# Two stages put in another order: the preparation of three weight sets before the image loop, and the third half band inside it

## The reference

```
x = x + wavelet_conv(group_norm(x), w0, w1, w2, bias)
x = x + similarity_conv(group_norm(x), spatial_weight)

wavelet_conv: three levels; each takes a 2x2 Haar transform of the low part,
  convolves the 128 stacked channels with its own 5x5 weights (128 x 128 x 25),
  and the inverse transforms add the levels up again
similarity_conv: a 5x5 neighbourhood; every neighbour is weighted by
  (cosine similarity over the channels + 1) / 2 * spatial_weight[tap]
```

## Time and profile before

| | us |
|---|---|
| median of 3 runs | 1970.23 |
| lowest and highest of them | 1963.1, 1977.1 |
| profiled execution | 1958.81 |
| its span, first to last instruction | 1957.2 |
| TensorE busy in it | 1624.4 (83%) |
| VectorE busy | 1364.0 (70%) |
| ScalarE busy | 748.6 (38%) |
| GpSimd busy | 428.0 (22%) |
| mean granted clock of TensorE | 0.915 of full speed |

### The profile page before, as it was taken

One profiled execution on the slowest core, in us unless ns is written; L12 is line 12 of the kernel. 1 busy time (PEld: TensorE's weight loads), 2 busy tenths in 40 slices (PEclk: granted clock), 3 DMA queues, 4 the chain that ended last, 5 costly groups with the idle time before them and its releaser, 6 DMA issues.

```text
span 1957.2 us, 52434 instructions
## 1 busy us (share of the span) xinstructions
PE 1624.4 (83%) x19071; PEld 884.2 (45%) x19071; DVE 1364.0 (70%) x1995; ACT 748.6 (38%) x1318; POOL 428.0 (22%) x760
## 2 busy tenths in 40 slices
PE   4868689799898889889888889888988888985686
PEld 3634244444444454444544444445444444442454
DVE  6433965986589766985599666985599557875553
ACT  2330135442445234432444244432544244423541
POOL 2333241302241222212040222212140223110000
PEclk8879889999999999999999999989999999897566
DMA  5332236755476626864576637673585547671664
GB/s 187 86 87 80 62 100 166 217 148 142 127 204 187 176 82 186 219 166 124 133 217 167 158 99 210 187 184 96 156 229 152 127 125 203 176 191 55 157 184 116
DMA packets 108649, 296.96 MB, mean 152 GB/s; under 512 B 24181, under 2 KB 57973, under 8 KB 107765
## 3 DMA queue, kind: packets, MB, share of 16 engines
q1 hardware_dynamic: 71408, 190.49, 36.9%
q0 software_dynamic: 36864, 101.47, 18.0%
HBM read 221.92 MB, written 69.94 MB: 149 GB/s over the span
## 4 chain that ended last, share of the span: by engine, by line
PE 49%; DVE 26%; issue 16%; ACT 5%; DVEq 2%; DMA 1%; POOL 1%; SPq 0%; ACTq 0%; POOLq 0%
PE conv L1283 13%; PE conv L1257 8%; PE gram L1348 8%; PE out_ps L1384 5%; DVE wgt L1019 4%; PE stat_ps L1306 4%; PE conv L1242 3%; PE vals_ps L1331 3%; PE out_ps L1373 2%; DVE st_s L970 2%; DVE st_a L967 2%; PE conv L1508 2%; DVE eo L835 2%; DVE xa L835 1%; DVE st_v L981 1%
## 5 line engine op out<-in xcount | busy, mean ns | idle before, releaser
L1283 PE MATMUL conv<-thl,wconv 128*128 128x496 f16 (+2 forms) x1920 | 514.8, 395 | 12.5 <-DVE xa L913 9.5
L1019 DVE SCALAR_TENSOR_TENSOR wgt<-gram,tapw 124x512 f32<-124x512 f32 x512 | 347.5, 682 | 224.2 <-PE gram L1348 189.2
L452 POOL DMA_DIRECT2D ring<-in_x x576 | 331.9, 582 | 340.1 <-ACT xa L524 251.0
L1348 PE MATMUL gram<-unit_mem 128*60 128x128 f16 x4096 | 251.5, 247 | 115.6 <-issue 54.8
L1348 PEld LDWEIGHTS gram<-unit_mem 128*60 128x60 f16 x4096 | 153.1, 113 | 321.2 <-issue 320.2
L1257 PE MATMUL conv<-thl,wconv 128*128 128x480 f16 (+7 forms) x1200 | 256.9, 368 | 0.0
L1283 PEld LDWEIGHTS conv<-thl,wconv 128*128 128x128 f16 x1920 | 159.3, 101 | 193.7 <-issue 39.4
L481 POOL DMA_DIRECT2D up<-d_z x128 | 69.3, 546 | 628.4 <-DVE xa L950 592.2
L524 ACT ACTIVATE thl<-tw 128x1024 f16<-128x1024 f32 x64 | 67.7, 1059 | 325.3 <-DVE tw L835 188.2
L1384 PE MATMUL out_ps<-wgt,vals 124*32 124x128 f32 x4096 | 182.1, 297 | 1.4 <-issue 0.8
L524 ACT ACTIVATE vals<-vals_ps 124x512 f32<-124x512 f32 x128 | 76.6, 598 | 258.5 <-PE vals_ps L1331 257.8
(11 more groups left out here) (140 smaller groups left out, 2073.1 us busy)
## 6 DMA issues: line engine op xcount, KB each, us to landing
unit_mem<-d_hl SPq DMA_DIRECT2D x128, 360.0 KB
unit_mem<-d_hl SPq DMA_DIRECT2D x256, 180.0 KB
ring<-in_x POOLq DMA_DIRECT2D x288, 128.0 KB, 2.7
ring<-in_x POOLq DMA_DIRECT2D x288, 127.0 KB, 2.8
d_hl<-st_hl SPq DMA_DIRECT2D x64, 360.0 KB
d_v<-st_v SPq DMA_DIRECT2D x64, 360.0 KB
unit_mem<-d_v SPq DMA_DIRECT2D x64, 360.0 KB
up<-d_z POOLq DMA_DIRECT2D x160, 128.0 KB, 2.6
```

The source lines that it names most:

```text
L452: pool.dma_start(dst, src).then_inc(raw_in[slot], 16)
L1019: V.scalar_tensor_tensor(out=dst, in0=g, scalar=SIM_SCALE ** 2, in1=tapw[:, :].unsqueeze(1).to_broadcast([KN, 2, 2 * QN]), op0=ALU.add, op ...
L1283: last = mm(dst[:, :, b0:b1], wconv0[:, w, 2 * (p % ROWS4) + s, dx + 2, :], thl[:, p % 2, d, s, :, b0 + dx:b1 + dx] if p % ROWS4 != 1 else ...
L1348: last = mm(bank[row:row + KQ, col:col + QN], key[:, q, e_at, TH * KW * g:TH * KW * g + KQ], tile[:, :, TH * g + 1:TH * g + 1 + TH, 1:1 + ...
```

## The change

- `wmix` is now three places: level 0's stays in `xa`, level 1's goes where `wraw[0]` lies, level 2's where `wraw[1]` lies. ScalarE writes into such a place once the raw weights there are mixed and their peak is found.
- TensorE's order becomes: one side of level 0, the first three tiles of its other side, one side of level 1, the other nine tiles of level 0, group-norm products of image 0, one side of level 2, levels 1 and 2 on the other side.
- VectorE's `peak(1)` moves behind level 0's first three tiles. The first four chunks' statistics move into level 0, the other four, the pad clearing and the group norm directly behind level 0, `peak(2)` behind these.
- ScalarE's `fill` of chunks 0 to 3 stands before level 2's half-mixed copies, `fill` of chunks 4 to 7 between the highs of levels 1 and 2. It waits for level 0's tiles alone.
- SP loads the tap table when level 1 is through (its place is level 1's half-mixed weights), instead of after level 0's first mix.
- In the loop ScalarE does `half_in` and `square_half` of half band 2 ahead of the copies of `up` and of half band 1's `count_own` and `unit_highs`, and three of the six norm pieces stand four to six matmuls later.

```diff
-NORMS_AT = [8, 20, 32, 50, 74, 92]
+NORMS_AT = [8, 20, 36, 54, 80, 92]
...
-        wmix = xa[:, :, :].rearrange("p a b -> p (a b)")[:, 0:TAPS * P]
-        wrow = [wmix[:, n * K * P:(n + 1) * K * P] for n in range(K)]
+        wmix = [xa[:, :, :].rearrange("p a b -> p (a b)")[:, 0:TAPS * P], wraw[0], wraw[1]]
+        wrow = [wmix[0][:, n * K * P:(n + 1) * K * P] for n in range(K)]
...
-            sp.wait_ge(wmixed, 7)
-            sp.wait_ge(wlevel, 1)
+            sp.wait_ge(wfull, TILES_BEFORE[2])
             sp.dma_start(tap_c, tapmask).then_inc(taps_in, 16)
...
                 if first(n):
-                    act.wait_ge(wfull, TILES_ALL)
+                    act.wait_ge(wfull, W0_TOTAL)
...
                     norms(b, 1, 0)
                     norms(b, 1, 1)
+                    half_in(b, 2)
+                    square_half(b, 2)
                 if conv:
 
                     act.wait_ge(up2_in, 64 * i + 64)
...
                     count_own(b, 1)
                     unit_highs(b, 1)
-                    half_in(b, 2)
-                    square_half(b, 2)
...
-            for n in range(3):
+            def keep_mixed(n):
                 for t in range(0, TAPS, 4):
                     m = min(4, TAPS - t)
                     k = 7 * n + t // 4
                     act.wait_ge(wmixed, k + 1)
                     if n > 0 and t == 0:
-                        act.wait_ge(wfull, TILES_BEFORE[n])
-                    copy(wmix[:, t * P:(t + m) * P], conv_ps[k % 2][:, 0:m * P]).then_inc(wmix_kept, 1)
+                        act.wait_ge(wlevel, 3 * n - 2)
+                    copy(wmix[n][:, t * P:(t + m) * P], conv_ps[k % 2][:, 0:m * P]).then_inc(wmix_kept, 1)
+
+            def highs(n, first_tile, end_tile):
...
+            keep_mixed(0)
+            highs(0, 0, 3)
+            keep_mixed(1)
+            highs(0, 3, W0_TOTAL)
+            root(gn1, gn1_var, gn1_root, 0)
+            for c in range(SLOTS):
+                fill(0, c)
+            keep_mixed(2)
+            highs(1, 0, 7)
+            for c in range(SLOTS, CHUNKS):
+                fill(0, c)
+            highs(2, 0, 7)
             act.wait_ge(const_in, 16 * 7)
-            root(gn1, gn1_var, gn1_root, 0)
-            for c in range(CHUNKS):
-                fill(0, c)
             opening(0)
...
+            level_scale(0)
...
+            dve.wait_ge(wmix_kept, 7)
+            combine(0, 0)
+            lows(0, tiles_of(0)[0:3])
+            peak(1)
+            combine(2, 1)
+            lows(0, tiles_of(0)[3:6])
+            dve.wait_ge(wfull, 6)
+            combine(3, 0)
+            for c in range(SLOTS):
+                raw_stats(0, c)
+            lows(0, tiles_of(0)[6:12])
+            level_scale(1)
+            dve.wait_ge(wfull, W0_TOTAL)
+            V.memset(xa[:, 0:2, :], 0.0)
+            V.memset(xa[:, H0 + 2:H0 + 4, :], 0.0)
+            V.memset(mean_conv, 0.0).then_inc(pads_clear, 1)
+            for c in range(SLOTS, CHUNKS):
+                raw_stats(0, c)
+            dve.wait_ge(const_in, 16 * 7)
+            gn_open(gn1, bn1, bn1_done, gn1_part, 0, CHUNKS)
+            gn_mean(gn1, gn1_chain, gn1_part, gn1_mm, 0)
+            gn_spread(gn1, gn1_mm, gn1_var, 0)
+            gn_close(gn1, gn1_chain, gn1_root, gn1_done, 0, X_SCALE)
+            peak(2)
+            level_scale(2)
+            lows(1, tiles_of(1))
+            lows(2, tiles_of(2))
...
+            mix_one_side(0)
+            level_products(0)
+            mix_both_sides(0, 0, 3)
+            mix_one_side(1)
+            mix_both_sides(0, 3, W0_TOTAL)
+            level_products(1)
             gn_products(gn1, gn1_part, gn1_mm, 0, 0)
             gn_products(gn1, gn1_part, gn1_mm, 0, 1)
+            mix_one_side(2)
+            level_products(2)
+            mix_both_sides(1, 0, 7)
+            mix_both_sides(2, 0, 7)
```

More of the change, by code:

```diff
@@ L738, in _ @@
                     if n > 0 and t == 0:
-                        act.wait_ge(wfull, TILES_BEFORE[n])
-                    copy(wmix[:, t * P:(t + m) * P], conv_ps[k % 2][:, 0:m * P]).then_inc(wmix_kept, 1)
+                        act.wait_ge(wlevel, 3 * n - 2)
+                    copy(wmix[n][:, t * P:(t + m) * P], conv_ps[k % 2][:, 0:m * P]).then_inc(wmix_kept, 1)
+            def highs(n, first_tile, end_tile):
                 act.wait_ge(wlevel, 3 * n + 3)
                 for k, (dst, scale) in enumerate(weight_tiles(n, 0), TILES_BEFORE[n]):
-                    act.wait_ge(wfull, k + 1)
-                    copy(dst, gram_ps[k % 2][:, 0:dst.shape[1]], scale=scale).then_inc(whigh, 1)
+                    if first_tile <= k - TILES_BEFORE[n] < end_tile:
+                        act.wait_ge(wfull, k + 1)
+                        copy(dst, gram_ps[k % 2][:, 0:dst.shape[1]], scale=scale).then_inc(whigh, 1)
+            keep_mixed(0)
[10 more added lines that the diff above has]
+            highs(2, 0, 7)
             act.wait_ge(const_in, 16 * 7)
-            root(gn1, gn1_var, gn1_root, 0)
-            for c in range(CHUNKS):
-                fill(0, c)
             opening(0)
@@ L1188, in _ @@
             peak(0)
-            for n in range(3):
-                level_scale(n)
-                if n == 0:
-                    dve.wait_ge(wlevel, 3)
-                    steps.link(dve, V.tensor_scalar(small[:, 7:8], wscale[0], 1 / 8, None, ALU.mult))
-                    steps.link(dve, V.tensor_scalar(small[:, 8:9], wscale[0], 1 / 32, None, ALU.mult))
-                    V.tensor_scalar(unscale_x, unscale[0], X_SCALE, None, ALU.mult)
-                    steps.link(dve, V.tensor_scalar(unscale_sq, unscale[0], unscale[0], None, ALU.mult))
-                if n < 2:
-                    peak(n + 1)
-                if n == 0:
-                    dve.wait_ge(wmix_kept, 7)
-                    combine(0, 0)
-                    lows(0, tiles_of(0)[0:3])
-                    combine(2, 1)
-                    lows(0, tiles_of(0)[3:6])
-                    dve.wait_ge(wfull, 6)
-                    combine(3, 0)
-                    lows(0, tiles_of(0)[6:12])
-                else:
-                    lows(n, tiles_of(n))
-                if n < 2:
-                    for c in range(SLOTS * n, SLOTS * n + SLOTS):
-                        raw_stats(0, c)
+            level_scale(0)
@@ new lines, in _ @@
+            dve.wait_ge(wlevel, 3)
+            steps.link(dve, V.tensor_scalar(small[:, 7:8], wscale[0], 1 / 8, None, ALU.mult))
+            steps.link(dve, V.tensor_scalar(small[:, 8:9], wscale[0], 1 / 32, None, ALU.mult))
+            V.tensor_scalar(unscale_x, unscale[0], X_SCALE, None, ALU.mult)
+            steps.link(dve, V.tensor_scalar(unscale_sq, unscale[0], unscale[0], None, ALU.mult))
+            dve.wait_ge(wmix_kept, 7)
+            combine(0, 0)
+            lows(0, tiles_of(0)[0:3])
@@ L1499, in _, with mix_one_side @@
             pe.wait_ge(zeroed, 4)
-            for n in range(3):
+            def mix_one_side(n):
                 w = wraw[n].rearrange("o (i t) -> o t i", t=TAPS)
@@ L1509, in _, with level_products @@
                     last.then_inc(wmixed, 1)
+            def level_products(n):
                 pe.wait_ge(wlevel, 3 * n + 1)
@@ L1516, in _, with mix_both_sides @@
                 last.then_inc(wlevel_mm, 1)
+            def mix_both_sides(n, first_tile, end_tile):
                 pe.wait_ge(wmix_kept, 7 * n + 7)
@@ L1521, in _ @@
                     sources = [(None, t) for t in range(0, TAPS, 4)]
-                for k, (kind, t) in enumerate(sources, TILES_BEFORE[n]):
+                for k, (kind, t) in enumerate(sources[first_tile:end_tile], TILES_BEFORE[n] + first_tile):
                     m = min(4, (TAPS if kind is None else 2 * K) - t)
@@ L1526, in _ @@
                     if kind is None:
-                        last = mm(gram_ps[k % 2][:, 0:m * P], mix, wmix[:, t * P:(t + m) * P], start=True, stop=True)
+                        last = mm(gram_ps[k % 2][:, 0:m * P], mix, wmix[n][:, t * P:(t + m) * P], start=True, stop=True)
                     elif kind == 1:
@@ L1531, in _ @@
                             at = s if s < K else (K - 1) * K + s - K
-                            last = mm(gram_ps[k % 2][:, (s - t) * P:(s - t + 1) * P], mix, wmix[:, at * P:(at + 1) * P],
+                            last = mm(gram_ps[k % 2][:, (s - t) * P:(s - t + 1) * P], mix, wmix[0][:, at * P:(at + 1) * P],
                                       start=True, stop=True)
```

8 lines of the change are left out of this document (removed).

## The result

| | before | after |
|---|---|---|
| median | 1966.66 (4 runs, 1952.63 to 1977.1) | 1903.92 (4 runs, 1897.99 to 1913.54) |
| ratio, 95% interval | | 0.971 (0.9642 to 0.9779) |
| profiled execution | 1958.81 | 1905.71 |
| its span | 1957.2 | 1904.2 |
| granted clock | 0.915 | 0.925 |

The change is faster by 2.9%. The direction was right and the size too small.

What follows compares the result with a forecast made beforehand. No engine alone sets the end (TensorE 49%, VectorE 26% of the chain of waits). Gains of 15 before the first image, 23.8 in seven iterations and 3.1 in iteration 8, 42 us, take 1970.2 to 1928, range 1914 to 1956.

Steps and rivals of the forecast that it cites:

- (a): Before the first image: `peak(1)` behind the first three low tiles brings TensorE's tile 2 to 28.9, gain 7.2 us.
- (b): Level 1's one-sided mix hides 11.3 us of VectorE, pays 2.2 us for low clock; TensorE back at level 0 at 44.1.
- (c): Rest of level 0 ends at 62, including 1 us for low clock; level scale and pads bring it to 63.8.
- (d): The second four chunks' reads start near 52.6, the last lands at 64.3; their four statistics end at about 66.3.
- (e): Group norm takes as long as before: first fill at 71.0; fill 3 awaits the ring's third read, ends at 77.1.
- (f): Level 2's one-sided mix, after a new wait behind ScalarE's copies and 1 us for the clock, ends at 87.0.
- (g): Other side of levels 1 and 2: level 1 until 96.8, fills 4 to 7 until 99.9, level 2 until 107.7.
- (h): Low-passes before the first image take 8.6, ending at 115.9; another 6.6 puts level 2's convolution at 122.5.
- Loop given back: Rival: the loop's eight steps are bound by VectorE and unit DMAs, 18 us of gain remain, 1952; chance 0.08.
- head nothing: Rival: the ring's third read and the ScalarE queue behind it swallow the gain before the first image, 1943; chance 0.08.
- Low clock throughout the head: Rival: one-sided mixes before the first image at half rate, head 15 us worse, loop 27 better, 1958; chance 0.06.
- ScalarE blocked at the new place of `half_in(2)`: Rival in the loop: ScalarE waits there on `unit_lows(0)`, some 12 us later than now, slower than before, 1990; chance 0.04.

Runs made afterwards that it cites:

- e5: The changed kernel with `peak(1)` back in front of level 0's first combination; 1919.07 us, ratio 0.98 to the kernel before.
- e2: The kernel before with only the loop's change, the old preparation kept; 1928.34 us, ratio 0.9863 to the kernel before.
- e8: The changed kernel, but SyncE loads unit 1 only when level 1's result is in memory (iterations 1 to 7); 1933.84 us, ratio 0.9897 to before.
- after_again: The repeat: the changed kernel measured once more, nothing altered; 1903.82 us, ratio 0.9743 to the kernel before.
- e10: The changed kernel with level 2's half-mixed copies ahead of fills 0 to 3 and the tap table's load behind chunk 7; 1900.16 us, ratio 0.9714 to before.
- e3: The changed kernel with the norm pieces at their old matmul numbers; 1910.20 us, ratio 0.9754 to the kernel before.
- e1: The changed kernel with the old loop, so only the new preparation before the first image; 1927.37 us, ratio 0.988 to the kernel before.
- e7: The changed kernel with ScalarE's half-mixed copies of level 2 ahead of fills 0 to 3; 1913.35 us, ratio 0.9793 to the kernel before.
- e4: The changed kernel with `half_in` and `square_half` of half band 2 at their old place; 1933.91 us, ratio 0.9898 to the kernel before.
- e9: The changed kernel with level 2's half-mixed copies ahead of fills 0 to 3 and the second count at matmul 131; 1912.00 us, ratio 0.9788 to before.
- e6: The changed kernel with group norm and all eight fills of image 0 behind the last weights; 1919.99 us, ratio 0.9812 to the kernel before.

## Why the prediction was right in kind and short in size

The miss is 1928 - 1903.9 = 24.1 us. Two steps make it. **The first that failed is the last of the sum, "that execution is 11.4 below the median", carried over to the changed kernel.** That distance came from a median of three. With eleven runs the median of before was 1954 to 1958, about where the profiled execution lay, and after's profiled execution is 1.8 above its median. This step alone puts the time outside the range: the lower end would have been 1914 - 11.4 = 1902.6 without it. The second is the gain. The profiled executions differ by 53.1, the forecast's sum was 42: 11.1 too small, 6.1 of it in the head (21.1 for 15), 2.2 in the loop with iteration 8 (29.1 for 26.9), and 2.6 in iteration 0 and behind step 0 of iteration 8, where the forecast had nothing. The rest of the miss, 1.6 us, is the 1.8 with rounding.

**The second step that failed is the head's sum, 15 instead of 21.1, and in it the clock terms.** Instant by instant (forecast, trace of after):

- (a) tile 2 at 28.9, trace 28.93; right, and e5 shows the price of undoing it, 7.8.
- (b) TensorE back at level 0 at 44.1, trace 41.77. The clock did fall (0.62 from 29.9 to 33), as I had it, but the 2.2 us weren't paid: the mix took 12.00 us, as the one of 12.08 in the earlier trace rows. The low rate in the window 36 to 40 of the earlier trace rows was that of other products, the level's other side, and I took it over to the mix.
- (c) VectorE reached the fifth chunk's statistics at 61.10, forecast 63.8: the distance held within 0.4, and the lead is that of (b). (d) the reads began at 51.38, forecast 52.6, and no statistic waited for one; the aggregate came at 63.70, forecast 66.3.
- (e) first fill 71.0, trace 67.47. One more us: the 4.7 of the group norm had the table load in it. It moved to 59.00, where nobody waits. But fill 3 waits for the ring, as said, and its end, 77.1 in the forecast and 74.7 in the trace, has only the lead of (b): the table load's 1 us was lost again there.
- (f) the new wait came, 5.32; the mix ended at 83.66 where I had 87.0, the 1 us for the clock again not there.
- (g) TensorE's last tile of level 2 at 107.3, trace 103.64: 19.3 us for both levels, forecast 19.6.
- (h) low-passes 8.6, trace 7.37, at 1.00 in the window. And behind them I kept the 6.6 us of before; it was 5.4, since after's third low-pass ran in 2.51 us (granted clock 0.79) and before's at 0.59 took

```profile
132.76 3.68 PE L1242 MATMUL conv<-sd,gat_c 128*128 128x256 f32 x8 [1.97 <-DVE thl L820]
```

  The clock term was missing there with the other sign.

Of the 6.2 us between 122.5 and 116.25, 2.3, 1 and 2.4 stand in (b), (f) and (h), all of them the clock's, and 0.3 in (g). My upper end for the head, 19, still held before's low rate in the last 6.6.

The Trainium skill's rule (TensorE: Matmul & The Clock Gate, HAM oscillation) would have made the head's gain 5. Its low clock was there behind the wait of 4.45 (0.62), but the burst behind it was no longer for it, and the alternation from 93 to 105, with waits up to 2.37 us, was granted 1.00. So the trace is against it as a price of this head. It doesn't contradict what the Trainium skill describes in that section: there each burst is shorter than the wait behind it, and in this alternation it is mostly longer. And some low clock came behind the instant where I cut: the first convolutions of after ran at 0.50, which cost 2.2 us of iteration 0 (last section).

**The loop was right in its sum and too small in its parts.** Forecast 23.8 for seven iterations and 3.1 for the last. e2, the loop alone, gives 27 us (19 to 35). In the traces the terms are 21.8 for six iterations (forecast 20.4; 17.6 in the repeat) and 7.3 for the seventh level part with iteration 8's (forecast 6.5). Piece 3's and 5's waits went, piece 6 came earlier, the second count kept its 0.66, as written. The level part gained 3.4 in iteration 2 and 3.6 to 4.3 in five others, the upper bound from both waits whole being 3.5; in iteration 1 it gained 7.2, since before's iteration 1 had the low clock twice (last section). Over iterations 1 to 6 that is 26.6 us, of which 21.8 reached the period (17.6 in the repeat, 25.0 in e2). Where the rest went I can't say: the steps' own spread is as large. The two things that rose are known. Level 1's result lands later, 7.3 to 8.8 us instead of 4.6 to 5.4, which e8 shows to be the collision with unit 1's load (the lower bound's case; its cost stayed hidden, since after_again and e10 have it too, with steps of 961.5 and 959.0 against 961.0 before). And TensorE waits longer in step 1 for nothing that the profile shows. The same thirteen matmuls of iteration 3, before and then after:

```profile
794.60 0.38 PE L1331 MATMUL vals_ps<-unpair_c,unit_mem 64*60 64x32 f16 x13 [1.19 <-issue]
```

```profile
761.17 0.55 PE L1343 MATMUL vals_ps<-unpair_c,unit_mem 64*60 64x32 f16 x13 [3.92 <-issue]
```

Over the loop such waits there came to 6.7 us in before and 19.2 in after, and to 9.5 to 14.8 in e2, e3 and the repeat. They may come with the late landing: in e8, which takes that back, they are 7.7. But they can't be what lengthens the steps, since e10 has 16.7 us of them and steps of 959.0. No run isolated them.

**The rivals.** Loop given back and head nothing: e2 and e1 exclude both. Low clock throughout the head: the two mixes took 12.0 and 8.4 us and the low-passes ran at 1.00. ScalarE blocked at the new place of `half_in(2)`: in iteration 2 of after neither piece 5 nor piece 6, which wait for what stands behind it, waits at all.

**The chances.** The interval was made of the edits' bounds. It let the clock terms go to nothing for the head only up to 19, where the trace has 21.1, and it left out that the execution's distance to the median could be nothing. Both should have been in it: 42 + 6 and 11 more reach 1911, and the runs' spread the rest.

## What to carry to other kernels

A wait that is moved must be followed to what it releases. Here e7 took away the 5.32 us wait that the profile showed, and its median gained nothing: the ring's reads then ended where a 1550 KB load began. One more wait on SyncE, on a load that nobody needed for 80 us, gave the lowest median of all. When the profile puts a wait down to "issue", look at how long the reads that it may stand behind took to land. A wait that is gone from one stage isn't time gained before the whole is measured: e4's level part was 8.9 us shorter than e1's and its time no better. Before the low clock is priced into a burst, look in a row of the same kind of matmul whether its pace follows the clock. And a forecast for a median should start from the profiled execution's own time unless there are enough runs to tell its distance to the median, since that distance is carried whole.

## What the runs showed of the hardware that I had not expected

- Fifty products of 128x128 in f32 with a weight load each took 12.00 us in after and in e5, with the granted clock at 0.62 and 0.66 for the first 3 us, and 12.08 in the earlier trace rows, where it was 1.00 (window 83.3 to 95.4). The 16 wider low-pass products took 7.37 us together at 1.00, and eight of them 6.09 at 0.61 (window 124.7 to 130.8 of before). One kind follows the clock, the other doesn't; what else sets the pace of the small ones no run shows.
- A bulk load delays other queues' small ones for long. The tap table was one issue of 0.34 us; with it under way for some 25 us, single reads of the ring took 10.7 us (e9) and 10.9 us (e6) to land, where the earlier trace rows have 3.7 at most. ScalarE's wait behind them was 8.12 and 11.42 us, and the profile puts such a wait down to "issue".
- The low clock can come in the middle of the loop. In iteration 1 of before, piece 5's wait of 2.71 was followed by

```profile
309.40:315.40 6.00, 6.00 (x20) 2.54 (x21) 0.00 (x0) 0.83 (x2) 0.00 (x0) 0.72 1.01 252
```

  and piece 6 came 6.08 us behind piece 5, where in iteration 2 it was 4.40 after the same wait. The same iteration's first convolutions were at the low clock too (0.66 from 279 to 285) and took 1.7 us more than iteration 2's; these two make its level part 3.3 us longer.
- The first convolutions behind the head were at the low clock in four executions (after, e5, e7 and e10, at 0.50 to 0.63) and at 1.00 in all others. The same stretch of 4.75 us in after and in after_again, the same kernel:

```profile
116.25:121.00 4.75, 4.75 (x26) 3.91 (x27) 4.68 (x3) 0.00 (x0) 0.00 (x0) 0.50 0.24 76
```

```profile
116.88:121.63 4.75, 4.75 (x49) 4.60 (x50) 4.68 (x3) 0.00 (x0) 0.00 (x0) 1.00 0.23 75
```

  26 products instead of 49 are some 2.2 us, an estimate from these two rows, and iteration 0 of after is 2.2 longer than that of after_again. In the 5 us ahead TensorE was busy for 2.5 us at 0.79 in after, and for 2.1 us at 1.00 in after_again. Why one execution gets the low clock and the next doesn't is open, for both stretches.
